# First steps of an attention stage: where the keys of the second unit and the values are projected

## What is computed

```python
# attention: query = layernorm(x), key = value = ctx
Q = split_heads(query @ Wq.T + bq)
K = split_heads(key @ Wk.T + bk)
V = split_heads(value @ Wv.T + bv)
scores = jnp.einsum('bhqd,bhkd->bhqk', Q, K) / np.sqrt(Hd).astype(jnp.float32)
attn = jax.nn.softmax(scores, axis=-1)
out = jnp.einsum('bhqk,bhkd->bhqd', attn, V)
...
x = x + out @ Wo.T + bo
x = x + ffn(layernorm(x))      # router, top 2 of 8, gate/up, clipped glu, down
```

## Time and profile before

| | us |
|---|---|
| three runs | 1777.14, 1781.18, 1782.4 |
| their median | 1781.18 |
| the profiled execution | 1776.77 |
| its span, first to last instruction | 1775.1 |
| TensorE busy | 1633.1 (92%) |
| VectorE busy | 1242.6 (70%) |
| GpSimd busy | 803.3 (45%) |
| ScalarE busy | 654.2 (37%) |
| mean granted clock of TensorE | 0.964 of 2.4 GHz |

### The profile page before, as it was taken

The page is one execution under the profiler, slowest core; times in us unless marked ns, Lnnn a source line. Parts: engine busy times, 40 slices in busy tenths (PEclk is TensorE's granted clock), DMA queues, the critical chain, the costliest instruction groups (busy, mean ns, idle before and its releaser), DMA issues. The chain is left out here.

```text
span 1775.1 us, 30007 instructions
## 1 busy us (share of the span) xinstructions
PE 1633.1 (92%) x9637; PEld 1178.9 (66%) x9637; DVE 1242.6 (70%) x2223; ACT 654.2 (37%) x1265; POOL 803.3 (45%) x619
## 2 busy tenths in 40 slices
PE   4798999999999999999997349999999999999996
PEld 3454555555555555555543149999999998999995
DVE  3566667776776777666673668777888778867874
ACT  3253444544445445344442123223333224222321
POOL 3255556555556565555665122333434333343422
PEclk9899999999999999999999559999999999999998
DMA  5332333343433434333321251334443245233422
GB/s 190 96 106 70 98 111 95 95 115 86 124 91 101 109 78 126 86 96 95 95 72 36 69 184 44 90 92 160 147 164 122 89 141 185 94 97 132 126 71 73
DMA packets 98804, 188.69 MB, mean 106 GB/s; under 512 B 26320, under 2 KB 27344, under 8 KB 98640
## 3 DMA queue, kind: packets, MB, share of 16 engines
q1 hardware_dynamic: 79408, 123.99, 24.7%
q0 software_dynamic: 19232, 62.73, 11.1%
HBM read 204.19 MB, written 37.36 MB: 136 GB/s over the span
## 5 line engine op out<-in xcount | busy, mean ns | idle before, releaser
L674 DVE TENSOR_REDUCE negmax<-max_ps 128x2 f32<-128x1024 f32 x256 | 312.4, 1220 | 207.6 <-PE max_ps L443 207.2
L563 ACT ACTIVATE pt<-work 128x512 f32<-128x512 f32 x512 | 278.7, 595 | 274.6 <-PE work L455 261.5
L757 POOL TENSOR_TENSOR acc<-acc,pt 128x1024 f32<-128x1024 f32 x128 | 303.4, 2372 | 134.6 <-ACT pt L563 133.8
L1292 PE MATMUL gu_ps<-xgT_hi,wg_hi 128*128 128x256 f32 x1248 | 355.1, 285 | 0.0
L1292 PE MATMUL gu_ps<-xgT_hi,wg_lo 128*128 128x256 f32 x1248 | 352.0, 282 | 0.0
L1292 PE MATMUL gu_ps<-xgT_lo,wg_hi 128*128 128x256 f32 x1248 | 351.6, 282 | 0.0
L754 POOL TENSOR_TENSOR acc<-pt 128x1024 f32<-128x1024 f32 x64 | 155.6, 2432 | 264.2 <-ACT pt L563 264.2
L1292 PEld LDWEIGHTS gu_ps<-xgT_hi,wg_hi 128*128 128x128 f32 x1248 | 235.7, 189 | 0.0
L1292 PEld LDWEIGHTS gu_ps<-xgT_lo,wg_hi 128*128 128x128 f32 x1248 | 235.7, 189 | 0.0
L1292 PEld LDWEIGHTS gu_ps<-xgT_hi,wg_lo 128*128 128x128 f32 x1248 | 235.5, 189 | 0.0
L443 PE MATMUL max_ps<-ks,qs 96*128 96x512 f32 x512 | 200.6, 473 | 24.3 <-DMA qs<-q_lo 15.4
(11 more groups left out here) (199 smaller groups left out, 2824.6 us busy)
## 6 DMA issues: line engine op xcount, KB each, us to landing
raw_g<-w_gate_up SPq DMA_DIRECT2D x39, 2048.0 KB
raw_d<-w_down SPq DMA_DIRECT2D x39, 1024.0 KB
ks<-k_hi SPq DMA_DIRECT2D x252, 64.0 KB, 2.0
qs<-q_hi SPq DMA_DIRECT2D x252, 64.0 KB, 2.0
bd<-b_down SPq DMA_DIRECT2D x39, 256.0 KB
x_in<-x SPq DMA_DIRECT2D x32, 256.0 KB, 3.1
ctxT_raw<-ctx_t SPq DMA_DIRECT2D x32, 256.0 KB, 4.0
x<-x SPq DMA_DIRECT2D x32, 256.0 KB, 2.9
```

Source lines behind the costliest of these rows:

```text
L563: e.activation(pt[k % 2][:, h, :], in_work("exp", u, k, h)[:, :], ACT.Exp, scale=scale).then_inc(exped.sem, 1)
L674: e.tensor_reduce(negmax[:, u % 2, n:n + 2], max_ps[:, :, :], AX.X, ALU.max, negate=True).then_inc(maxed.sem, 1)
L757: e.tensor_tensor(acc[:, heads, :], acc[:, heads, :], pt[k % 2][:, heads, :], ALU.add).then_inc(added.sem, 1)
L1292: ins = e.matmul(gu_ps[n % GU_BANKS][:, part, :], wg[s][pw][:, k, cols], xgT[s][px][:, k, :], start=(k == 0 and m == 0), stop=(k == KD - 1 ...
```

## The change

The orders of steps -2 and -1 are written anew. The keys of unit 1 are projected in step -2, directly behind the queries of unit 0, and not in rounds 1 and 2 of step -1. The queries of unit 1 move to rounds 0 and 1 of step -1, from rounds 3 and 4. The two value tiles of unit 0 move from round 0 to rounds 2 and 3, and those of unit 1 from rounds 5 and 6 to 4 and 5. The splits of `wv` move one round later, behind `k_hi` of unit 1 on ScalarE and ahead of `k_lo` of unit 1 on VectorE. No instruction is added or dropped; one blank line shifts the line numbers behind it by one.

```diff
@@ -196,16 +196,17 @@
                     at(0, ("k", u, 0), ("k", u, 1))
                     at(1, ("low", u, "k"))
                     at(2, ("q", u, 0), ("q", u, 1))
-                    at(3, ("low", u, "q"), *[("split", "v", k) for k in range(C)])
+
+                    at(3, ("low", u, "q"), ("k", 1, 0), ("k", 1, 1))
+                    at(4, *[("split", "v", k) for k in range(C)], ("low", 1, "k"))
                 elif s == -1:
-                    at(0, ("v", 0, 0), ("v", 0, 1))
-                    at(1, ("v_out", 0, 0), ("v_out", 0, 1), ("k", u, 0))
-                    at(2, ("k", u, 1))
-                    at(3, ("low", u, "k"), ("q", u, 0))
-                    at(4, ("q", u, 1))
-                    at(5, ("low", u, "q"), ("v", u, 0))
-                    at(6, ("v_out", u, 0), ("v", u, 1))
-                    at(7, ("v_out", u, 1))
+                    at(0, ("q", u, 0))
+                    at(1, ("q", u, 1))
+                    at(2, ("low", u, "q"), ("v", 0, 0))
+                    at(3, ("v_out", 0, 0), ("v", 0, 1))
+                    at(4, ("v_out", 0, 1), ("v", u, 0))
+                    at(5, ("v_out", u, 0), ("v", u, 1))
+                    at(6, ("v_out", u, 1))
```

## The result

| | before | changed |
|---|---|---|
| median of six runs, us | 1780.49 | 1771.9 |
| lowest and highest | 1777.14, 1782.4 | 1770.67, 1775.03 |
| ratio to before, 95% interval | | 0.9956 [0.9944, 0.9968] |
| span of the profiled execution, us | 1775.1 | 1769.0 |

The change makes the kernel faster by 0.44% (0.32% to 0.56%), or 7.8 us by the ratio and 8.6 by the medians. The forecast was 1773.8 us in a range of 1769.5 to 1779, and a gain of 7.4. Faster by more than 0.3% had a chance of 0.76.

What follows compares the result with a forecast made beforehand. SyncE's queue of issues was taken to bound the start: +0.7 - 1.08 - 6.8 - 0.2 = -7.4 us, from 1776.77 to 1769.4 profiled. With 4.4 us added for a median the forecast was 1773.8 us, range 1769.5 to 1779.

Steps and rivals of the forecast that it cites:

- What bounds the start: SyncE's queue of issues, 43.84 to 61.34 us, not TensorE's work; unit 0's row maxima wait 6.83 us in it.
- Keys into the first hole, at no cost: In TensorE's 7.27 us hole after unit 0's queries, unit 1's 12 key matmuls run from 26.3 to 29.3 at no cost.
- Contention: GpSimd's q_lo copies of unit 0, now beside SyncE's copies, land later: first pair from 34.00 to 34.7, +0.7 us.
- The eight rounds: Unit 0's maxima, first to eighth pair: 16.40 us instead of 17.48, first round 3.95; -1.08 us.
- Maxima out of the queue: SyncE's queue: unit 0's maxima copies wait 0.02 us before issue instead of 6.83; -6.8 us.
- From issue to exponents: From issue of unit 0's maxima copies to the first exponent matmul: 4.12 us instead of 4.32; -0.2 us.
- What is late next: Before the exponent matmul: TensorE still idles about 2 us, waiting for the maxima's round trip.
- A: First hole: the clock survives, first round 2.07 us instead of 3.95; gain 9.3 us, 1771.9; chance 0.12.
- B: Just before the exponents: the clock falls on dense work, price 1.9 us; gain 5.5 us, 1775.7; chance 0.13.
- C: First hole: SyncE's copies served ahead of GpSimd's q_lo, 6.4 us lost; gain 1.0 us, 1780.2; chance 0.05.
- D: After the start: later waits for copies absorb the gain, 1781.2 us; chance 0.06.
- E: Rounds two to six: the clock does not come back, 1.88 us each; 2.0 us slower, 1783.2; chance 0.04.

Runs made afterwards that it cites:

- The two halves of the change: On the kernel before: unit 1's keys alone into the first hole, 0.9999, again 0.9993; or only the order keys, queries, values inside step -1, 0.998.
- the second profile of the same kernel: The changed kernel itself, unaltered, run and profiled once more: ratio 0.9953 to the kernel before.
- the spread order with filled rounds: Changed kernel with unit 1's queries also in the first hole, values in rounds 0, 2, 4, 6, five idle matmuls in rounds 1, 3, 5, 7: 0.9925.
- spread: Changed kernel with unit 1's queries also in the first hole and the values in rounds 0, 2, 4 and 6: ratio 0.9925.
- bunched: Changed kernel with unit 1's queries also in the first hole and the values in rounds 0 to 3: ratio 0.995.

## Why the prediction was right, by its steps

*What bounds the start* was right: the queue of issues, and not TensorE's work. The two halves of the change show it from both sides.

*Keys into the first hole, at no cost*: right. They ended at 28.97, forecast 29.3, from a start that was 0.5 us early.

*Contention* (+0.7): from the beginning of GpSimd's `q_lo` issues to the first pair 4.00 us passed (30.05 to 34.05), before 3.48: 0.5 us. The copies took 2.3 us instead of 2.1:

```profile
qs<-q_lo POOLq DMA_DIRECT2D x4, 64.0 KB, 2.3
```

The two effects that the Trainium skill speaks of, interleaving on the same DMA engines (DMA: Bandwidth & Descriptors, "Issuing engines are not separate DMA queues") and turns between the queues ("Queues, rings and completion order"), agree with this trace: the neighbours cost 0.5 us and did not hold the copies back by 6.

*The eight rounds* (-1.08): mis-sized. They took 17.31 us, forecast 16.40. I had the clock back after 3.7 us of work, as before; it took 5.6 us (34.05 to 39.7), so the rounds came to 0.9 us more: the second had 3.16 us and the third 2.33 instead of 2.07 each; the first had 3.62, forecast 3.95. (Of the six rounds behind the first, only one has no projection, not two as I wrote; it kept its length, 2.05 us.) In the second profile of the same kernel the rounds took 16.47 us, with the second at 2.46: the forecast's value. The term scatters between executions by nearly 1 us, and I gave it no such range.

*Maxima out of the queue* (-6.8): measured 6.80. The number was right and its account too narrow. I wrote it as the maxima's wait alone; with ScalarE issuing them it disappears and the kernel gains nothing, because the queries' copies were equally late. The sum held since the change moves both.

*From issue to exponents* (-0.2): mis-sized. 4.32 us before, 2.99 now, so -1.33. I had taken the wait one unit later, 4.12 us, as the normal case. The two copies of the maxima took 1.8 and 1.9 us to land here:

```profile
qs<-m_hi SPq DMA_DIRECT2D x1, 8.0 KB, 1.8
qs<-m_lo SPq DMA_DIRECT2D x1, 8.0 KB, 1.9
```

Before, they had taken 3.3 and 3.6, right behind four loads of 256 KB each. With these loads issued behind the maxima, and nothing else changed, they took 1.9 each:

```profile
qs<-m_hi SPq DMA_DIRECT2D x1, 8.0 KB, 1.9
```

Now the last load is out 2.5 us ahead of them. That the 3.3 and 3.6 came from the loads follows. The 4.12 us one unit later do not come from this: no load is ahead there, `m_hi` took 1.8 us and `m_lo` 3.4, and the query copies directly ahead are no reason, since in the run above they stood directly ahead too. What held this one `m_lo` up is open; in the changed kernel it took 1.9 at the same place.

The three errors (-0.2, +0.9, -1.1) come to -0.4 us, and the start was 0.5 us early, so the first exponent was at 57.51 against a forecast of 58.3. That a gain of 7.4 was forecast and 7.8 measured rests in part on this cancelling, which was luck; the large term was right by itself.

*What is late next*: wrong in its detail. TensorE does not wait 2 us in front of the exponents. It comes just in time, since the clock fell at 53.4 and what stands in front of them ran at half speed for most of its length.

*The rivals.* A (the clock survives the first hole) did not happen, but filling the hole made it happen and gained 2.4 us (2.1 from the first pair), where I had priced it at 1.9. B (the clock falls before the exponents) did happen. The price shows in the time from the issue of `m_hi` to the first exponent: 2.57 us in the spread order with filled rounds, where the clock stayed up, 2.99 in the first profile, where it was low from 53.4 to 56.8, and 3.63 in the second, where it was low until 59.9. So it cost 0.4 and 1.1 us up to the first exponent, and was priced at 1.9. The prediction also misread the kernel before: there the lower level did not end with the wait, but at 65.0, after 4.2 us of work. It cost nothing there only because the maxima's copies were late anyway. The Trainium skill (TensorE: Matmul & The Clock Gate, "HAM oscillation — how this bites in real kernels") expects a cold start behind each wait for a DMA: the trace agrees for the hole of 5 us. At the sparse end of the rounds the clock fell too, but no wait there is longer than 1.41 us, and none is for a DMA. C, D and E did not happen: `q_lo` was 0.5 us late and not 6.4; 7.7 of 8.15 us arrived at the expert stage; and the clock came back within two rounds.

## What to carry to other kernels

Where two engines wait for DMAs of one queue, look at when the *first* of the block of issues could start, not at the transfer that is late: 24 issues of 0.6 us are 15 us. Starting the first of them 12.8 us earlier (31.05 instead of 43.84) brought 8 us; moving the four loads behind the maxima brought nothing. Before costing a removed wait in full, look for a second user of the same queue that is late by as much; curing one of two equal waits gave 0.2 us of 6.8. And spread filler work over the rounds of a loop that another engine paces: the same work in the same eight rounds was 1.6 us faster spread than bunched, by one trace of each.

## What the runs showed of the hardware that was not expected

- A small copy (8 KB) right behind four large loads in the same queue landed in 3.1 to 4.2 us (four traces), in 2.9 to 3.0 with 0.8 us between, and in 1.8 to 1.9 with 2.5 us between or with the loads behind it.
- TensorE's clock fell inside a loop in which it was never idle for longer than 1.3 us at a stretch: two rounds of 2.05 us with nothing but a 0.73 us pair each, behind dense work until 42.4, and it fell at 46.4 us, just as the third began.
- The same kernel had its lower clock behind the same hole for 5.6 us of work in one profile and 3.8 in another, and one execution had a low stretch of 3.4 us (44.2 to 47.6) that the other profile of the same kernel did not have. Terms of this size can't be forecast better than to 1 or 2 us from one trace.
